# Linear attention with routed experts: a table load moved into the first phase, and lane one-hots made tile by tile

## The reference

```python
q = elu(xn @ Wq.T) + 1;  k = elu(xn @ Wk.T) + 1;  v = xn @ Wv.T     # 16 heads of 8
kv = einsum('bnhd,bnhm->bhdm', k, v);  k_sum = k.sum(axis=1)
attention = (q @ kv / (q @ k_sum + 1e-6)) @ Wo.T
aff = xn @ centroids.T;  assign = argmax(aff)                       # 8 experts, one for each token
alpha = sigmoid(aff[assign])
h = relu(layernorm(xn, ln_g[e], ln_b[e]) @ w1[e].T + b1[e])
ffn = alpha * (xn + h @ w2[e].T + b2[e]) + (1 - alpha) * xn         # e = assign
```

## Time and profile before

| | us |
|---|---|
| median of 3 runs | 155.09 (155.02 to 155.37) |
| the profiled execution, its own time | 155.4 |
| its span | 153.6 |
| busy: PE, DVE, ACT, POOL | 138.0, 111.8, 101.4, 115.4 |

### The profile page before, as it was taken

The page is one execution under the profiler, slowest core; times in us unless marked ns, Lnnn a source line. Parts: engine busy times, 40 slices in busy tenths (PEclk is TensorE's granted clock), DMA queues, the critical chain, the costliest instruction groups (busy, mean ns, idle before and its releaser), DMA issues.

```text
span 153.6 us, 4729 instructions
## 1 busy us (share of the span) xinstructions
PE 138.0 (90%) x1138; PEld 131.5 (86%) x1138; DVE 111.8 (73%) x395; ACT 101.4 (66%) x334; POOL 115.4 (75%) x137
## 2 busy tenths in 40 slices
PE   3945999896999999999999999999999999999930
PEld 3945898796988998899999999999999999999920
DVE  3999998999968988897856554667777756556440
ACT  7533988999448786886666657666666666666610
POOL 7644430899958867888887768878888888877774
PEclk9999999999999999999999999999999999999997
DMA  4999200499937999677678998877777777841111
GB/s 142 327 323 420 94 4 0 151 344 294 274 89 214 241 340 286 163 201 192 161 195 233 287 338 205 216 190 207 196 166 174 189 160 174 135 41 53 51 51 51
DMA packets 26601, 29.10 MB, mean 189 GB/s; under 512 B 3024, under 2 KB 20432, under 8 KB 26448
## 3 DMA queue, kind: packets, MB, share of 16 engines
q1 hardware_dynamic: 21808, 23.69, 49.9%
q0 software_dynamic: 4480, 5.05, 17.8%
q10 hardware_dynamic: 288, 0.07, 0.2%
HBM read 18.18 MB, written 10.62 MB: 187 GB/s over the span
## 4 chain that ended last, share of the span: by engine, by line
PE 72%; POOL 9%; DVE 7%; ACT 5%; DMA 3%; issue 2%; SPq 1%; DVEq 0%
PE bank L718 22%; PE bank L706 21%; PE bank L671 6%; POOL out L417 5%; PE bank L688 5%; PE bank L659 4%; POOL feat_k L425 4%; PE bank L596 3%; DVE stats L770 3%; DMA x<-in_x 3%; PE bank L679 3%; PE bank L698 2%; PE bank L651 2%; DVE xn L818 2%; ACT k_exp L510 2%
## 5 line engine op out<-in xcount | busy, mean ns | idle before, releaser
L541 ACT ACTIVATE hT<-bank,b 128x128 f32<-128x128 f32 x156 | 44.6, 369 | 25.8 <-PE bank L706 25.7
L718 PE MATMUL bank<-w,hT 128*128 x312 | 42.8, 280 | 0.8 <-ACT hT L541 0.7
L706 PE MATMUL bank<-zT,feat_k 128*128 128x128 f32 x312 | 41.2, 275 | 0.0
L718 PEld LDWEIGHTS bank<-w,hT 128*128 128x128 f32 x312 | 37.8, 191 | 2.0 <-issue 1.2
L706 PEld LDWEIGHTS bank<-zT,feat_k 128*128 128x128 f32 x312 | 37.9, 192 | 0.0
L409 POOL DMA_INDIRECT out<-rows,token_at x20 | 32.0, 1602 | 6.1 <-issue 6.1
L396 POOL DMA_INDIRECT rows<-z_rows,token_at x20 | 20.6, 1030 | 5.0 <-issue 3.5
L1037 DVE TENSOR_SCALAR zT<-xn,ln_g,ln_b 128x128 f32 x39 | 14.2, 363 | 9.6 <-issue 8.7
L1052 DVE SCALAR_TENSOR_TENSOR rows<-y_own,weight,rows 128x128 f32 x39 | 13.8, 355 | 7.8 <-DVE y_own L1044 5.8
L425 POOL TENSOR_TENSOR feat_k<-feat_k,k_exp 128x256 f32<-128x256 f32 x16 | 14.2, 908 | 7.0 <-ACT k_exp L510 6.4
L396 POOL DMA_INDIRECT rows<-z_base_rows,token_at x12 | 12.0, 1000 | 4.0 <-issue 3.4
(11 more groups left out here) (124 smaller groups left out, 256.9 us busy)
## 6 DMA issues: line engine op xcount, KB each, us to landing
feat_k<-in_w1T SPq DMA_DIRECT2D x39, 256.0 KB, 4.1
z_rows<-xn SPq DMA_DIRECT2D x4, 528.0 KB, 5.0
z_base_rows<-xn SPq DMA_DIRECT2D x8, 264.0 KB, 5.4
x<-in_x SPq DMA_DIRECT2D x8, 256.0 KB, 4.8
w<-in_w2T SPq DMA_DIRECT2D x1, 2048.0 KB, 10.4
out<-x SPq DMA_DIRECT2D x8, 256.0 KB
z_base_rows<-x SPq DMA_DIRECT2D x16, 128.0 KB
b<-in_b SPq DMA_DIRECT2D x1, 512.0 KB, 5.8
```

Of the source, the lines that this page charges most:

```text
L541: last = a.activation(hT[:, par, c * P:(c + 1) * P], bank[hidden_bank(s)][:, c * P:(c + 1) * P], ACT.Relu, bias=b1[:, c, bass.ds(e, 1)])
L706: last = t_.matmul(bank[hidden_bank(s)][:, c * P:(c + 1) * P], w1_now[:, s % W1_RING * FC + c, :], zT[:, s % ZT_RING, :], start=True, stop ...
L718: last = t_.matmul(bank[y_bank(s)][:, 0:D], hT[:, par, c * P:(c + 1) * P], w2[:, bass.ds(e * (FC * D) + c * D, D)], start=(c == 0), stop=( ...
```

## The change

Five things, in one diff:

- ACT's exponential table is loaded in the values phase, after `copy_v(1)`, and batch 0 of the keys gets its exponentials there. DVE computes 1/std of the last chunk, and 1/std of the second norm, without ACT: from a guess made on the number's bits, with three Newton rounds, both in one set of operations on 44 columns (`rsqrts_of_both`).
- The choice of experts is made in three parts (16, 8 and 8 tiles) in place of two; `ranks` stands behind `keys_values(0)`; `tokens` stands behind `keys_values(10)` in place of `keys_values(9)`.
- The lane table is gone. Each tile's lane one-hot is a `tensor_scalar` that compares one row of 128 lane numbers (f16) with the tile's number, a [128, 1] scalar: 32 operations of 128 x 128 in place of four of 128 x 1024.
- `staircase` and `words` move from the key phase into steps 1 and 2 of the attention loop. PE, ACT and DVE wait for `expert_ready` at step 10 only; SP waits where it did.
- `EARLY` goes from 20 to 18, and `UNSCATTERED` from 27 to 26.

```diff
-    LANE_PARTS = 4
-    CHOOSE = (0, 16, 32)
+    CHOOSE = (0, 16, 24, 32)
-    TOKENS_AT = 9
+    TOKENS_AT = 10
-    EARLY = 20
-    UNSCATTERED = 27
+    EARLY = 18
+    UNSCATTERED = 26
...
+        lane_hot = sb("lane_hot", [P, NT, P], f16)
...
-            expand_lanes(0)
...
             copy_v(0)
             copy_v(1)
+            a.activation(warm[:, :], mean[:, 0:1], ACT.Exp, scale=0.0)
+            exp_of_k(0)
             for gr in range(2, NG + LAG):
...
-                    if b == 2:
-                        sqrt_of(2)
-                        sqrt_of_second()
-            a.activation(warm[:, :], mean[:, 0:1], ACT.Exp, scale=0.0)
...
-            exp_of_k(0)
+            exp_of_k(1)
             act.wait_ge(max_ready, len(CHOOSE) - 1)
             a.activation(alpha_e[:, :], aff_max[:, :], ACT.Exp, scale=-1.0).then_inc(sig_exp, 1)
-            for b in range(1, NB):
+            for b in range(2, NB):
                 exp_of_k(b)
...
+                for r in range(ROUNDS):
+                    step(v_.tensor_tensor(sq[:, 0:n + NT], guess[:, 0:n + NT], guess[:, 0:n + NT], ALU.mult), filling)
+                    step(v_.tensor_tensor(nw[:, 0:n + NT], sq[:, 0:n + NT], halved[:, 0:n + NT], ALU.mult), filling)
+                    if r < ROUNDS - 1:
+                        step(v_.scalar_tensor_tensor(guess[:, 0:n + NT], nw[:, 0:n + NT], 1.5, guess[:, 0:n + NT], ALU.add, ALU.mult),
+                             filling)
...
-                v_.tensor_tensor(lane_hot[:, :, part], lane_neg[:, :, part], lo_neg[:, part].unsqueeze(1).to_broadcast([P, P, TH]),
-                                 ALU.is_equal).then_inc(lane_ready, 1)
+                for t in range(h * TH, (h + 1) * TH):
+                    last = v_.tensor_scalar(lane_hot[:, t, :], lane_row[:, :], lo_neg[:, t:t + 1], None, ALU.is_equal)
+                last.then_inc(lane_ready, 1)
...
             hot_lanes(0)
+            mask_kv(0)
             hot_lanes(1)
             hot_lanes(2)
-            mask_kv(0)
             hot_lanes(3)
             mask_kv(1)
-            staircase()
+            slot_tokens()
             mask_kv(2)
-            words()
-            slot_tokens()
             mask_kv(3)
...
+                if j == 1:
+                    staircase()
+                if j == 2:
+                    words()
                 if j == WORDS_AT:
+                    dve.wait_ge(expert_ready, 1)
                     steps.word(0)
```

More of the change, by code:

```diff
@@ L101, in linear_attention_and_routed_experts @@
         ones = sb("ones", [P, P], bf16)
-        lane_neg = sb("lane_neg", [P, P, NT], f16)
-        lane_row = sb("lane_row", [P, P], bf16)
+        lane_row = sb("lane_row", [P, P], f16)
         tile_start = sb("tile_start", [P, NT, NT], f16)
@@ L124, in linear_attention_and_routed_experts @@
         rstd = sb("rstd", [P, NT])
-        var_2, var_2_half, std_2, rough_2, sq_2, nw_2, rstd_2 = (
-            sb(n, [P, NT]) for n in ("var_2", "var_2_half", "std_2", "rough_2", "sq_2", "nw_2", "rstd_2"))
+        raised, halved, guess, sq, nw = (sb(n, [P, NT + TC]) for n in ("raised", "halved", "guess", "sq", "nw"))
+        rstd_2 = sb("rstd_2", [P, NT])
         spread = sb("spread", [P, NT])
@@ L462, in copy_xnT @@
                 a.activation(xnT[:, gr * TG * P:(gr + 1) * TG * P], bank[gr % 2][:, :], ACT.Copy).then_inc(xnT_ready, 1)
-            def expand_lanes(q):
-                some = slice(q * P // LANE_PARTS, (q + 1) * P // LANE_PARTS)
-                a.activation(lane_neg[:, some, :], lane_row[:, some].unsqueeze(2).to_broadcast([P, P // LANE_PARTS, NT]), ACT.Copy)\
-                 .then_inc(lane_full, 1)
             def copy_v(b):
@@ L510, in exp_of_k @@
                 a.activation(k_exp[:, part, :], k_neg[:, neg, :], ACT.Exp, scale=-1.0).then_inc(k_exp_ready, 1)
-            exp_of_k(0)
+            copy_xnT(0)
+            copy_xnT(1)
+            sqrt_of(1)
+            copy_v(0)
+            copy_v(1)
+            a.activation(warm[:, :], mean[:, 0:1], ACT.Exp, scale=0.0)
+            exp_of_k(0)
+            for gr in range(2, NG + LAG):
+                if gr < NG:
+                    copy_xnT(gr)
+                for j in range(TG // TB):
+                    b = (gr - LAG) * TG // TB + j
+                    if b not in V_BY_DVE:
+                        copy_v(b)
+            exp_of_k(1)
             act.wait_ge(max_ready, len(CHOOSE) - 1)
             a.activation(alpha_e[:, :], aff_max[:, :], ACT.Exp, scale=-1.0).then_inc(sig_exp, 1)
-            for b in range(1, NB):
+            for b in range(2, NB):
                 exp_of_k(b)
@@ L638, in tokens @@
                         pe.wait_ge(lane_ready, t // TH + 1)
-                    last = t_.matmul(bank[TOKENS][:, 0:NT], lane_hot[:, :, t], tile_val[:, :, t],
+                    last = t_.matmul(bank[TOKENS][:, 0:NT], lane_hot[:, t, :], tile_val[:, :, t],
                                      start=(t == 0), stop=(t == NT - 1))
@@ L812, in rsqrts, with rsqrts_of_both @@
                 dve.wait_ge(rstd_ready, c + 1)
+            def rsqrts_of_both(filling):
+                part = slice(CHUNK[NCH - 1], NT)
+                n = NT - CHUNK[NCH - 1]
+                dve.wait_ge(var_ready, NCH)
+                v_.tensor_scalar(raised[:, 0:n], var[:, part], EPS_LN, None, ALU.add)
+                step(v_.tensor_scalar(raised[:, n:n + NT], var[:, :], 1.0 + EPS_LN, EPS_LN * EPS_LN, ALU.mult, ALU.add), filling)
+                v_.tensor_scalar(halved[:, 0:n + NT], raised[:, 0:n + NT], -0.5, None, ALU.mult)
+                step(v_.tensor_scalar(guess[:, 0:n + NT].bitcast(i32), raised[:, 0:n + NT].bitcast(i32), -0.5, SEED, ALU.mult, ALU.add),
+                     filling)
[4 more added lines that the diff above has]
+                        step(v_.scalar_tensor_tensor(guess[:, 0:n + NT], nw[:, 0:n + NT], 1.5, guess[:, 0:n + NT], ALU.add, ALU.mult),
+                             filling)
+                v_.scalar_tensor_tensor(rstd[:, part], nw[:, 0:n], 1.5, guess[:, 0:n], ALU.add, ALU.mult).then_inc(rstd_ready, 1)
+                step(v_.scalar_tensor_tensor(rstd_2[:, :], nw[:, n:n + NT], 1.5, guess[:, n:n + NT], ALU.add, ALU.mult), filling)
+                dve.wait_ge(rstd_ready, NCH)
             def normalise(c):
@@ L846, in _ @@
             moments(2, rows_1, rows_1)
-            next(rows_1)
-            dve.wait_ge(var_ready, NCH)
-            v_.tensor_scalar(var_2[:, :], var[:, :], 1.0 + EPS_LN, EPS_LN * EPS_LN, ALU.mult, ALU.add).then_inc(var_2_ready, 1)
-            rsqrts(2, rows_1)
+            rsqrts_of_both(rows_1)
             finish(rows_1)
@@ L854, in second_norm @@
             def second_norm():
[L856 to L863 removed]
+                step(v_.scalar_tensor_tensor(spread[:, :], var[:, :], EPS_LN, rstd[:, :], ALU.add, ALU.mult), nothing)
                 v_.tensor_tensor(xn[:, :, AT_C], spread[:, :], rstd_2[:, :], ALU.mult).then_inc(meta_ready, 1)
@@ L962, in _ @@
             choose(0)
+            second_norm()
             copy_v(V_BY_DVE[0])
-            second_norm()
+            choose(1)
             for b in V_BY_DVE[1:]:
                 copy_v(b)
-            for c in range(1, len(CHOOSE) - 1):
-                choose(c)
+            choose(2)
             dve.wait_ge(const_ready, 8)
```

46 lines of the change are left out of this document (9 added, 37 removed).

## The result

| | before | changed |
|---|---|---|
| median of the runs, us | 155.23 (155.02 to 156.49, 4 runs) | 163.38 (162.42 to 164.48, 4 runs) |
| profiled execution, us | 155.4 | 162.42 |
| its span, us, and mean granted clock | 153.6, 0.995 | 160.3, 0.967 |

The ratio of the medians is 1.0509, with a 95% interval of 1.0415 to 1.0604: slower, as forecast (160.2 us), but 2.0 us above the top of the range (161.4).

The account below looks back on a forecast made before the run. POOL, not PE, was taken to end the kernel, fixed by the attention phase's end. 155.4 + 2.9 + 1.1 + 1.2 = 160.6; the median 0.3 lower, 160.3, forecast as 160.2 us; range 153.8 to 161.4.

Parts of the forecast that it names:

- Where the bound lies: Whole kernel: POOL ends it, with fixed work of 70.05 us from its first `z_base_rows` gather, which waits for a store.
- one for one: Attention phase to kernel end: any shift of the attention phase moves the end by the same time.
- The table load and the early batch: ACT's idle from 12.72 us: load, warming and key batch 0 fit, saving 1.28 + 0.1 + 0.85 us later; `copy_xnT(2)` not late.
- What DVE pays for it: Values phase: last chunk's 1/std at 19.2 us, 1.3 us late; choice ends about 28.1, but nothing ends later up to there.
- The lane one-hots: Key phase: 32 small DVE compares stall behind POOL's running sums, delaying the first `num`; +2.9 us, ends -1.7 and +3.2.
- The attention loop: Attention steps 1 and 2: staircase and words give DVE 2.0 to 2.7 us more; +1.1 us, ends 0 and +2.1.
- EARLY: POOL behind the wait for `zb_out`: two more gathers, two scatters whole instead of adding; +1.2 us, ends -1.2 and +1.2.
- The three terms of the sum: Added to the profiled execution before: lane one-hots +2.9, staircase and words in the attention loop +1.1, EARLY 18 +1.2 us.
- Rival D: Key phase: ending the large lane operations frees POOL, `num` starts at about 42.8; faster, 153.9 us; chance 0.22.

## Why the forecast was right in kind and short in size

- **Where the bound lies**: right. POOL ends both kernels, and behind the first gather from `z_base_rows` it has no wait longer than 0.71 us. That a shift of the attention phase goes through "one for one" holds only roughly: with the table back the first `num` is 3.6 us earlier and POOL's end 4.2; with the row in PSUM the first `num` is 3.5 later and the end 1.6; with the mask first it is 0.9 later and the end 0.8 earlier.
- **The table load and the early batch**: right. The load is at 12.54 us, and `copy_xnT(2)` starts at 14.95 (15.22 before), not late. No drain shows; the next operation starts 0.02 us behind the load's end:

```profile
12.54 1.28 ACT L485 ACT_TABLE_LOAD   x1
13.84 0.20 ACT L485 ACTIVATE warm<-mean 128x1 f32<-128x1 f32 x1
```

- **What DVE pays for it**: 1/std starts at 18.99 us and the nine tiles at 19.30; group 5 is on PE at 20.34, with 0.87 us idle. All are near the forecast's 19.2 and 20.6. The choice ended at 28.7 and not 28.1, and so the compares began at 35.30 and not 34.8.
- **The lane one-hots**: the mechanism right, 0.68 us apart beside sums and 0.1625 free, as the forecast had (0.70 and 0.16). The experiment with the row in PSUM shows what the stall hangs on, the one with the table its price of 3.6 us. That the net +2.9 met 2.99 is partly luck: the compares began 0.5 us later than forecast, and one stall of 0.5 us fewer came at the end (POOL's last sum started at 44.33, behind the last compare), so they ended at 44.21 for 44.4. The working of that term also doesn't add up as it stands: PE's tokens were to end 3.3 us later (44.9 for 41.62), not the 3.6 that it writes, and 3.3 less 0.45 is the 2.9 that it uses, not 3.15.
- **The attention loop**: +1.24 for +1.1, and confirmed by putting it back. That SP's stores catch up by their third was wrong: they did by the fifth (69.83 us), which still cost nothing.
- **EARLY**: +1.24 for +1.2, and confirmed. The three terms of the sum together came to 5.47 us for 5.2.
- **The step that failed is the sum, in the term that it left at nothing.** It has nothing for the path between the sixth `num` and the first gather from `z_base_rows`, taken as fixed. That path gave 0.18 + 0.34 + 0.69 = 1.2 us, and what lies outside the span 0.3. The forecast had the gather wait for the last store, rightly, but took the time that this wait lasts from the one trace of before. From the start of the last store's issue to the gather it is 3.8 us before, 4.5 after, and between 3.3 and 5.4 over the ten other kernels that leave SP's stores in their order; I take it for scatter and can't show a cause.
- **The second error was the median.** I took it 0.3 under the profiled execution, as before had it; here it is 0.96 above, since the profiled execution was the fastest of the four. Of the 3.2 us between 160.2 and 163.38, the three terms have 0.3, the path 1.2, what lies outside the span 0.3, and the median 1.3; 0.1 is the forecast's rounding. So the range, whose top met only the tops of the terms, had no room for either. Rival D, at 0.22, pulled the bottom down and not the top up. Why the runs of the changed kernel scatter over 2.1 us stays open. Its mean granted clock is 0.956 to 0.967, and the slowest two have the lowest, 0.956, but four runs are too few to call that the cause, and in the profiled one about two thirds of the time at half clock lies in the last 7 us, where PE does nothing at all.

## What to carry to other kernels

Before one large VectorE operation is cut into many, look what GpSimd does in that stretch: in this kernel a small operation on SBUF tensors waited there for what GpSimd's running instruction had left, so the number of operations counted more than their size. Where its tensor came from PSUM it didn't wait. A row of the profile in which a small operation takes the neighbour's duration (0.69 us for 128x32) is worth more than a table of unit costs. And a chain that "goes through one for one" can have a scatter of its own at a DMA that it crosses, here 3.3 to 5.4 us for the same store; that belongs in the range, and the one trace of before may stand at its low end.

## What the runs showed of the hardware

- Where PE had been dry in this stretch (3.61 us changed, 2.34 and then three shorter waits with the mask first, 5.49 with the compares alone, 2.16 and then 3.31 with the row in PSUM) the granted clock fell to 0.50, that is 1.2 GHz, for some microseconds, and four matmuls took 1.06 us where they take 0.61. With the table back, after one wait of 0.91 us, it stayed at 1.00; with sums half as wide it fell too, after three shorter waits (0.54, 0.35, 0.91), so the length of one wait isn't all that counts. Where the slow stretch lay under DVE's compares, as in the changed kernel, the way from the tokens to the first `num` took the 3.0 us that it takes at full clock; behind them it took up to 1.6 more (4.65). None of my terms had it.
- A DVE compare of 128 x 128 to f16 starts its neighbour after 0.1625 us from f16 in SBUF, 0.20 as f32 `tensor_tensor`, and 0.258 from f32 in PSUM; the last alone ran on evenly beside GpSimd's sums.
- A compare and a sum that both want SBUF took turns: the compare ended with the running sum (0.72 to 0.76 us, or 0.45 to 0.55 beside half sums), and a sum that met a row of `tensor_tensor` compares stood until they were through (2.47 us in place of 0.72).
- SP's issue of the same two stores took 1.01 us in one kernel and 2.03 in another.
